# The last expert group's zeros and weights are issued by ScalarE instead of SyncE, and the steps' places are drawn anew

## The chip, the cores and the metric

The kernel runs on one core of a Trainium2 chip. The metric is the device time of one execution in microseconds (us); lower is better. The median of three runs of the kernel before is 5308.69 us (5287.12 to 5310.76).

The engines are called by their names in the profile: PE (TensorE, matmuls and transposes; PEld is its weight load), DVE (VectorE), ACT (ScalarE), POOL (GpSimd) and SP (SyncE, which only issues DMAs here). SPq and ACTq are the DMA issues of SyncE and ScalarE.

## The reference

An input x of 32 batches of 512 tokens with 256 features goes through a Mamba layer with an MLP, a layer norm, a mixture of 8 experts with the best 2 for each token and one shared expert, and a second layer norm, all in float32:

```python
def step(h, inp):                       # the scan of the Mamba layer, 16 states, 512 channels
    dt_t, B_t, C_t, x_t = inp
    dA = jnp.exp(dt_t[..., None] * A)
    h = dA * h + (dt_t * x_t)[..., None] * B_t[:, None, :]
    y = jnp.einsum('bdn,bn->bd', h, C_t)
    return (h, y)
...
h = x + _mamba(_layernorm(x, norm1_g, norm1_b), ...)
m = _layernorm(h, norm2_g, norm2_b)
attn = h + jax.nn.gelu(m @ mlp_w1.T + mlp_b1, approximate=False) @ mlp_w2.T + mlp_b2
x = _layernorm(x + attn)
...
scores = jax.nn.softmax(xf @ gate_w.T, axis=-1)
_, idx = jax.lax.top_k(scores, 2)       # each token's two experts, weighted by their scores
h = jax.nn.silu(g) * u                  # g and u: x times wg and wu of an expert
routed = ...                            # h times wd of the two experts, weighted and summed
shared = jax.nn.silu(xf @ sg.T) * (xf @ su.T) @ sd.T
x = _layernorm(x + routed + shared)
```

## The kernel before

**The order of the work.** Each engine runs one queue in program order. The work on an engine is cut into strands, generators such as `pre`, `scan`, `weigh`, `post`, `experts`, `results`, `finish` and `last`, each of which yields before each of its steps the batch to which the step belongs. `weave` (L99) merges the strands of an engine into one order by places: a step has the place 64 x batch + its entry of the table `AT` (L22), and never less than the place of the strand's step before. The tables are constants in the source. They hold for every batch, so an entry that moves does so in all 32. Places only order the steps of one engine; between the engines, semaphores decide.

**One batch** (512 tokens) goes through these steps. `pre`: sums and squares of x (ACT L698, L684), GpSimd's `normed` (L561) which gives less, ve, rs and nb of a norm, normalised tokens, their transposes, the first half of in_proj, the convolution (DVE L1218), silu, x_proj (B, C and the rank of dt), dt. B goes to DRAM (`B_rows`, L417) and comes back broadcast, one DMA for each of the 16 states (`B_spread`, L423). `scan`: for each state and each quarter of the channels, 64 times a batch, ACT computes exp(dt A) into PSUM (L755), POOL dt x B into dBx (L600, two quarters at a time), DVE runs the scan (L1229) into hs. `turn` and `weigh`: PE transposes hs into one of two PSUM banks (L974), DVE multiplies with C and adds to acc (L1245; for two of the sixteen states ACT, L768). `post`: the gate z (L991; its tanh L777, its product on DVE L1278), the sum y (L1004, L1007), w_out (L1019, L1021), mid norm, w_m1 (L1037), gelu, w_m2 (L1054), norm, the transposes of its output (L1062), the gate of the experts (L1068), the routing on DVE (L1293 to L1361), the shared expert, whose output and residual go to the DRAM buffer `shared` (ACT L825, L830), and the scatter of the tokens' rows to their experts' places in DRAM (`X_slots`, POOL L633, four indirect DMAs for the first expert and four for the second).

**The experts.** Batches form groups of 6, 6, 6, 6, 4, 2, 1 and 1 batches. When a group is scattered, `group_tiles` on DVE (L1392) writes the tiles' expert and row (`where`) and each expert's end (`ends`), 18 increments of `s_meta`. `pad` on SyncE (L434) waits for these and writes zeros behind the rows of each of the 8 experts, to an address read from `ends` into a register (L443). `all_rows` (L445) waits for the scatters and the zeros. The group's tiles of 128 rows are worked in pairs: `experts` on SyncE loads the weights (wx, L499) and the rows (xin, L505) of a pair, PE turns the rows (L1112), ACT copies them (xsT, L842), PE multiplies (L1130), ACT takes tanh (L847), DVE the products (L1373, L1376), PE the second matmul (L1145), ACT the scaled output (L858), SyncE stores it to `Y_slots` (L521). A batch has up to 12 slots for pairs (`pairs_in`); in batches 5 to 22 four or five of them are filled, with five the third slot among them.

**The finish** of a batch f needs its group's pairs done. SyncE loads `shared[f]` into the single buffer fx (L534), after waiting until batch f-1 is stored; POOL gathers the two experts' outputs into it with adding (L657, 4 and 4); ACT sums, squares and scales (L895, L684, L902) with POOL's `normed` between, and stores fx to the output (L905). The finishes of batches 27, 28 and 29 lie in the period of batch 30, those of 30 and 31 behind it.

**The last group** is batch 31 alone, with 16 tiles in 8 pairs (152 to 159, here 0 to 7). They have a buffer each (`wx_last`, `xin_last`), made of tiles that are free at the end. `last` on SyncE (L449) is one strand of 24 steps: 8 steps for the weights, the first of them with `pad` and waits for the last scans and transposes ahead; 8 for the rows, the first with `all_rows`; 8 for the outputs. `last` on PE (L1149), ACT (L861) and DVE (L1378) works the pairs staggered: the turn of a pair, the up step of the one before, the down step of the one before that. The lines of its steps are L1166, L871, L1175, L875, L1383, L1386, L1183 and L880. SyncE's loop over weights in `last` is:

```python
for q in range(NLAST):
    yield b
    if q == 0:
        pad(g)
        sp.wait_ge(s_scan, NB * STEPS)
        sp.wait_ge(s_y_turned, NB * CT)
    if q < 2:
        sp.wait_ge(s_down_e, P0 - 1 + q)
    ...
```

Of the kernel before, what the change touches and what calls it, by code (L numbers as in the profile page):

```python
# [9 lines left out]
def group_sizes(n):  # L10
# [6 lines left out]
    while n:  # L17
# [4 lines left out]
AT = {  # L22
    "ACT_experts": [124.46, 125.74, 128.8, 130.54, 134.61, 135.95, 138.86, 140.84, 142.27, 142.38, 143.71, 144.95,
        147.84, 148.99, 151.85, 153.09, 159.61, 160.41, 161.35, 163.09, 166.53, 167.41, 170.1, 171.48],
    "ACT_finish": [152.12, 152.3, 152.3, 152.68, 152.68, 152.68, 152.77, 152.92, 154.73, 155.55, 156.25, 157.25,
        167.31, 167.41, 167.41, 167.72, 167.72, 168.27, 168.27, 169.78, 170.2, 170.5, 170.5, 170.72, 197.59, 197.59,
        197.59, 197.59, 199.29, 199.63, 199.63, 199.63, 200.22, 200.22, 200.49, 200.79],
    "ACT_last": [137.32, 137.32, 137.42, 137.51, 137.53, 137.86, 139.07, 139.77, 139.77, 139.77, 139.77, 139.77,
        139.77, 140.66, 140.66, 140.66, 151.62, 151.62, 151.62, 151.86, 151.86, 151.86, 151.86, 151.86, 152.02,
        152.58, 153.06, 159.5, 162.22, 166.33, 190.88, 194.43],  # L30
    "ACT_post": [57.1, 59.75, 64.53, 68.94, 78.62, 78.62, 79.9, 80.49, 81.18, 81.28, 81.28, 81.28, 84.15, 84.15,
        84.15, 84.57, 86.17, 86.17, 87.39, 87.76, 88.72, 89.94, 97.56, 97.76, 97.76, 97.94, 99.44, 101.28, 102.72,
        103.29, 104.47, 106.02, 110.38],
    "ACT_pre": [-63.04, -63.04, -59.75, -59.75, -57.63, -54.43, -50.92, -50.92, -48.17, -32.48, -32.48, -32.48,
        -32.23, -32.01, -31.14, -25.59, -24.16, -21.01, -19.09, -15.37, -13.12, -11.61, -10.78, -8.01, -6.93, -2.89],
    "ACT_results": [126.79, 127.91, 132.04, 132.47, 136.47, 136.47, 141.6, 141.6, 142.98, 142.98, 145.52, 145.96,
        150.28, 151.15, 159.16, 159.18, 160.57, 160.89, 165.97, 165.97, 168.69, 169.98, 183.41, 185.11],
    "ACT_scan": [1.69, 3.47, 6.65, 7.28, 7.82, 7.96, 8.71, 9.61, 9.71, 10.72, 12.65, 12.65, 13.91, 14.57, 15.17,
# [4 lines left out]
    "ACT_weigh": [8.02, 10.28, 10.28, 11.04, 35.16, 36.34, 37.2, 38.03],  # L43
    "DVE_experts": [126.01, 129.67, 137.46, 140.93, 144.44, 146.06, 148.7, 153.41, 161.62, 163.32, 169.38, 174.12],
    "DVE_last": [121.51, 127.93, 156.82, 165.91, 166.45, 166.45, 183.01, 191.57],
    "DVE_meta": [106.25, 108.81, 109.84, 109.84],
    "DVE_post": [55.59, 56.79, 64.86, 67.56, 71.93, 74.38, 74.81, 75.03, 93.66, 97.97, 97.97, 97.97, 98.09, 102.46,
        103.96, 104.39, 104.39, 104.39, 104.39, 104.39, 104.39, 105.62, 105.62, 108.47],
    "DVE_pre": [-29.44, -27.59, -27.59, -25.26, -25.26, -25.26, -21.68, -21.68, -21.68, -19.08, -19.08, -18.92],
    "DVE_scan": [2.28, 3.93, 6.98, 7.82, 10.46, 10.46, 10.46, 10.46, 10.76, 11.11, 15.72, 15.72, 17.24, 17.24, 17.69,  # L50
# [4 lines left out]
    "DVE_weigh": [15.86, 16.54, 16.71, 17.85, 19.73, 19.73, 19.73, 19.73, 19.73, 19.73, 20.22, 22.1, 22.1, 25.31,  # L55
# [15 lines left out]
    "PE_turn": [8.63, 9.5, 10.6, 10.97, 11.04, 14.67, 15.36, 16.7, 19.29, 19.29, 19.87, 19.87, 20.8, 21.29, 21.32,
# [45 lines left out]
def build(nc, a, out):  # L117
# [4 lines left out]
    P = 128  # L122
# [59 lines left out]
    with ctx:  # L182
# [200 lines left out]
        def _(sp):  # L383
# [1096 lines left out]
```

## Time and profile before

| | us |
|---|---|
| median of three runs | 5308.69 |
| lowest and highest | 5287.12, 5310.76 |
| the profiled execution | 5320.7 |
| its span | 5318.9 |
| DVE busy | 4398.7 (83%) |
| PE busy | 4254.3 (80%) |
| POOL busy | 3584.5 (67%) |
| ACT busy | 3387.0 (64%) |
| DMA, mean rate | 106 GB/s |

The profile is of one execution, whose own time is 5320.7 us. A row of the timeline gives the start in us, the duration, the engine, the line, the operation, the written and the read tile, and how many instructions are merged; in brackets stands the idle time of the engine before it and what ended it. A row of the waits gives who waited for whom, the total in us, how many times, and the longest. A row of the windows gives for each engine its busy time in a stretch, the granted clock of TensorE (1 is full speed), the mean busy share of the 16 DMA engines and what they moved. Releasers are inferred from semaphores; where no one is seen, "issue" stands.

### The profile page before, as it was taken

To read this page: it belongs to the slowest core of one execution; us is meant where nothing else is said; L and a number is where in the kernel's file an instruction comes from. 1 tells how busy PE (TensorE), PEld (TensorE's weight loads), DVE (VectorE), ACT (ScalarE), POOL (GpSimd) and SP (SyncE) were. 2 spreads that over 40 slices of the span, in tenths; PEclk is the share of its full clock that TensorE was granted. 3 is DMA by queue.
4 is the path that set the end of the run, shared out by engine and by line. 5 is a ranking of instruction groups with operands and counts; after the bars stand their busy time and mean duration, and the time that the engine had idled before them with its cause. 6 is when DMAs were issued, how large, how long until landed. Compare 5 with 4: busy or idle time off the path is not lost. (4 is left out here: it accounts for less than half of the span.)

```text
span 5318.9 us, 75837 instructions
## 1 busy us (share of the span) xinstructions
PE 4254.3 (80%) x20928; PEld 2954.7 (56%) x20928; DVE 4398.7 (83%) x6313; ACT 3387.0 (64%) x6338; POOL 3584.5 (67%) x2252
## 2 busy tenths in 40 slices
PE   3777888788888888888888888888888888888872
PEld 2455555565555556555555655555555566655652
DVE  4899988988888988888888888888888888888841
ACT  4666666566666666766666766666666766766642
POOL 4666666666666667776667776667777775787743
PEclk7899998999999999989998998999998999999986
DMA  1224232233333333333233333333344442555655
GB/s 63 71 70 112 71 95 86 86 128 119 106 121 98 123 124 89 93 96 107 83 84 85 105 98 104 92 84 96 80 126 116 117 122 92 151 147 141 166 141 153
DMA packets 357156, 563.53 MB, mean 106 GB/s; under 512 B 40433, under 2 KB 203378, under 8 KB 356610
## 3 DMA queue, kind: packets, MB, share of 16 engines
q1 hardware_dynamic: 286082, 457.85, 28.2%
q0 software_dynamic: 49152, 67.27, 6.2%
q10 hardware_dynamic: 21504, 33.56, 1.7%
q8 instruction: 174, 2.85, 0.2%
q14 instruction: 244, 2.00, 0.1%
HBM read 440.66 MB, written 186.05 MB: 118 GB/s over the span
## 5 line engine op out<-in xcount | busy, mean ns | idle before, releaser
L600 POOL TENSOR_TENSOR dBx<-dtx,Bbc 128x1024 f32<-128x1024 f32 x1024 | 2431.3, 2406 | 728.6 <-DVE hs L1229 666.3
L1229 DVE TENSOR_TENSOR_SCAN hs<-ps,dBx 128x512 f32<-128x512 f32 x2048 | 2389.3, 1205 | 206.7 <-ACT ps L755 104.9
L755 ACT ACTIVATE ps<-dt,A 128x512 f32<-128x512 f32 x2048 | 1391.5, 689 | 576.6 <-DVE hs L1229 548.0
L974 PE MATMUL ps<-ident,hs 128*128 128x128 f32 x8192 | 1341.2, 304 | 507.2 <-DVE acc L1245 392.8
L974 PEld LDWEIGHTS ps<-ident,hs 128*128 128x128 f32 x8192 | 1029.3, 154 | 982.1 <-DVE acc L1245 641.1
L1245 DVE SCALAR_TENSOR_TENSOR acc<-ps,C_tok,acc 128x512 f32<-128x512 f32 x1792 | 1281.6, 738 | 284.3 <-PE ps L974 266.2
L657 POOL DMA_INDIRECT fx<-Y_slots,slots x256 | 405.0, 1582 | 126.7 <-issue 67.9
L633 POOL DMA_INDIRECT X_slots<-xs,slots x256 | 257.4, 1005 | 290.3 <-DVE slots L1361 231.9
L1130 PE MATMUL ps<-xsT,wx 128*128 128x128 f32 x2432 | 321.2, 282 | 65.0 <-ACT xsT L842 65.0
L1130 PEld LDWEIGHTS ps<-xsT,wx 128*128 128x128 f32 x2432 | 301.1, 195 | 112.7 <-issue 108.8
L1218 DVE SCALAR_TENSOR_TENSOR xc<-ps,conv_w,xc 128x511 f32<-128x511 f32 (+2 forms) x384 | 285.4, 744 | 63.5 <-ACT xc L719 50.6
L991 PE MATMUL ps<-xnT,w_in 128*128 128x512 f32 x512 | 295.7, 684 | 0.9
L939 PE MATMUL ps<-xnT,w_in 128*128 128x512 f32 x512 | 271.9, 648 | 25.9 <-DVE xc L1218 25.0
L584 POOL TENSOR_TENSOR dt<-dt,dtx 128x1024 f32<-128x1024 f32 x64 | 152.4, 2381 | 173.1 <-ACT dtx L746 173.1
L1054 PE MATMUL ps<-w_m,post_tmp 128*128 128x256 f32 x1024 | 261.8, 390 | 0.0
L1021 PE MATMUL ps<-w_out,xc 128*128 128x256 f32 x1024 | 250.4, 380 | 0.0
L1037 PE MATMUL ps<-mT,w_m 128*128 128x512 f32 x512 | 239.6, 600 | 11.1 <-ACT mT L798 10.6
L719 ACT ACTIVATE xc<-ps,conv_b,conv_w 128x512 f32<-128x512 f32 x128 | 99.0, 773 | 204.1 <-PE ps L939 201.5
L963 PE MATMUL ps<-few 16*128 16x512 f32 x256 | 181.1, 796 | 52.4 <-ACT dt L741 39.3
L1145 PE MATMUL ps<-wx,ge 128*128 128x256 f32 x608 | 171.5, 406 | 55.3 <-DVE ge L1376 53.3
L1054 PEld LDWEIGHTS ps<-w_m,post_tmp 128*128 128x128 f32 x1024 | 196.6, 197 | 27.0
L1021 PEld LDWEIGHTS ps<-w_out,xc 128*128 128x128 f32 x1024 | 192.7, 191 | 25.0
(210 smaller groups left out, 5888.2 us busy)
## 6 DMA issues: line engine op xcount, KB each, us to landing
Bbc<-B_scratch SPq DMA_DIRECT2D x512, 256.0 KB
wx<-in_experts SPq DMA_DIRECT2D x308, 384.0 KB, 5.0
Y_slots<-zeros SPq DMA_DIRECT2D x228, 256.0 KB, 4.6
xin<-X_slots SPq DMA_DIRECT2D x308, 128.5 KB, 4.1
Y_slots<-xin SPq DMA_DIRECT2D x308, 128.0 KB
xt<-in_x SPq DMA_DIRECT2D x32, 512.0 KB, 5.2
shared<-xt ACTq DMA_DIRECT2D x32, 512.0 KB
fx<-shared SPq DMA_DIRECT2D x32, 512.0 KB
```

Of the source, the lines that this page charges most:

```text
L600: pool.tensor_tensor(dBx[u % 3][:], dtx[b % 2][:, 2 * h:2 * h + 2, :], Bbc[g % NBB][:, n % CH:n % CH + 1, :].broadcast_to([P, 2, T]), ALU. ...
L657: pool.indirect_dma_start(out=fx[:, t, :], out_offset=None, in_=Y_slots[g % 2], in_offset=bass.IndirectOffsetOnAxis(ap=slots[:, f % NKEPT, ...
L755: act.activation(psA[s % 2][:], dt[b % 2][:, j, :], ACT.Exp, scale=A[:, j, n:n + 1]).then_inc(s_dA, 1)
L939: i = pe.matmul(bank(b, j)[:], w_in[:, k, j * P:(j + 1) * P], xn[:, k, :], start=(k == 0), stop=(k == KD - 1))
L974: i = pe.transpose(psH[w % 2][:, j * P:(j + 1) * P], hs[(n * CT + j) % NHB][:, t * P:(t + 1) * P], ident[:])
L991: i = pe.matmul(psG[j % 2][:], w_in[:, k, DI + j * P:DI + (j + 1) * P], xn[:, k, :], start=(k == 0), stop=(k == KD - 1))
L1021: i = pe.matmul(psG[q][:, t * D:(t + 1) * D], c[:, k, (2 * q + t) * P:(2 * q + t + 1) * P], w_out[:, k, :], start=False, stop=(k == CT - 1))
L1054: i = pe.matmul(psG[q][:, t * D:(t + 1) * D], post_tmp[:, k, (2 * q + t) * P:(2 * q + t + 1) * P], w_m2[:, k, :], start=False, stop=(k == ...
L1130: i = pe.matmul(psE[:, o * HALF + m * P:o * HALF + (m + 1) * P], w[:, m, (2 * k + o) * P:(2 * k + o + 1) * P], xsT[:, (m * KD + k) * P:(m ...
L1218: dve.scalar_tensor_tensor(out=c[:, j, s:], in0=bank(b, j)[:, 0:T - s], scalar=conv_w[:, j, NK - 1 - s:NK - s], in1=c[:, j, s:], op0=ALU.m ...
L1229: dve.tensor_tensor_scan(hs[s % NHB][:], psA[s % 2][:], dBx[s // 2 % 3][:, s % 2, :], 0.0, ALU.mult, ALU.add).then_inc(s_scan, 1)
L1245: dve.scalar_tensor_tensor(out=o, in0=psH[w % 2][:], scalar=C_tok[b % 2][:, t, n:n + 1], in1=o, op0=ALU.mult, op1=ALU.add).then_inc(s_weig ...
```

## The change

The eight weight steps of the last group leave SyncE's strand `last`, which keeps the 8 steps for the rows and the 8 for the outputs. A new strand `issue_last` on ScalarE issues the zeros and the weights of the eight pairs, with the waits that they had on SyncE (for the metadata, the last scans and transposes, and for the pairs whose buffers are taken over). The waits of `pad` for the first two groups aren't needed there. The first row step on SyncE keeps `all_rows`. DMAs, sizes and semaphores are the same.

```diff
@@ SyncE, last() @@
                 for q in range(NLAST):
                     yield b
                     if q == 0:
-                        pad(g)
-                        sp.wait_ge(s_scan, NB * STEPS)
-                        sp.wait_ge(s_y_turned, NB * CT)
-                    if q < 2:
-                        sp.wait_ge(s_down_e, P0 - 1 + q)
-                    for i in range(2):
-                        e = sp.value_load(where[g % 2][0:1, 1, 2 * q + i:2 * q + i + 1], min_val=0, max_val=NE * P)
-                        sp.dma_start(wx_last[q][:, i, :], a["experts"].rearrange("e p f -> (e p) f")[
-                            bass.ds(e, P), :]).then_inc(s_wx_last[q], 16)
-                for q in range(NLAST):
-                    yield b
-                    if q == 0:
                         all_rows(g)
@@ ScalarE @@
+            def issue_last():
+
+                g, b = NG - 1, NB - 1
+                for q in range(NLAST):
+                    yield b
+                    if q == 0:
+                        act.wait_ge(s_meta, NG * NMETA)
+                        for e in range(NE):
+                            r = act.value_load(ends[g % 2][0:1, e:e + 1], min_val=0, max_val=ROWS - P)
+                            act.dma_start(X_slots[g % 2][bass.ds(r, P), :], zeros[:, 0:ROW]).then_inc(s_padded[g % 2], 16)
+                        act.wait_ge(s_scan, NB * STEPS)
+                        act.wait_ge(s_y_turned, NB * CT)
+                    if q < 2:
+                        act.wait_ge(s_down_e, P0 - 1 + q)
+                    for i in range(2):
+                        e = act.value_load(where[g % 2][0:1, 1, 2 * q + i:2 * q + i + 1], min_val=0, max_val=NE * P)
+                        act.dma_start(wx_last[q][:, i, :], a["experts"].rearrange("e p f -> (e p) f")[
+                            bass.ds(e, P), :]).then_inc(s_wx_last[q], 16)
...
-                  (finish(), AT["ACT_finish"]), (last(), AT["ACT_last"]))
+                  (finish(), AT["ACT_finish"]), (last(), AT["ACT_last"]), (issue_last(), AT["ACT_issue_last"]))
```

All tables of `AT` have new entries. In most strands an entry moves by less than a tick or two (a batch has 64, so a tick is some 2.5 us in the loop). Those that move more: ACT_post's last entry, the shared part's last copy and its store, from 110.38 to 118.35; SP_clear's, most of which lie at 91 to 99 before and spread from -27 to 67 after; SP_B_spread's and SP_experts', by up to 14 and 10; the tables of the last group. The new table is

```python
    "ACT_issue_last": [108.86, 108.86, 113.58, 125.48, 127.66, 129.33, 129.33, 138.47],
```

From the tables the new orders follow. At the end, ScalarE has after the store of batch 28: the zeros with the weights of pairs 0, 1 and 2; the shared part's last copy and store; pair 0's copy; the weights of pairs 3 to 6; pair 0's tanh; the first pass of batch 29's finish over one tile; pair 1's copy; one output of pair 0; the rest of batch 29's finish with its store; the weights of pair 7; the other output of pair 0, and pairs 1 to 6 except for one output; batch 30's finish with that output inside; pair 7's tanh and outputs. SyncE has: fx for batch 29; the rows of pair 0; the output of pair 151; the rows of pairs 1 and 2; fx for batch 30; the rows of pairs 3 to 7; the outputs of pairs 0 to 6; fx for batch 31; the output of pair 7.

In the loop, around the steps that the prediction speaks of (places within a batch):

```
ScalarE before: scan 0, 1 | sums 2, 3 of x | tanh 3 | a square | xsT of the third slot | scan 2
ScalarE after:  scan 0, 1 | xsT of the third slot | sum 3 of x | tanh 3 | scan 2, 3 | a square
GpSimd before:  dBx 7 | rs_pre | gathers 0 to 3 | dBx 8, 9 | less_mid
GpSimd after:   dBx 7 | gathers 0, 1 | dBx 8 | rs_pre | gathers 2, 3 | dBx 9 | less_mid
TensorE before: turn 43 | turn of C, dt 0, 1 | turns 44 to 47
TensorE after:  turns 43, 44 | turn of C, dt 0, 1 | turns 45 to 47
VectorE before: weighing 35 | scans 49 to 51 | weighings 36, 37, 38
VectorE after:  weighings 35, 36 | scans 49 to 51 | weighings 37, 38
```

## Rows read from the trace of the kernel before

**Rows 1.** The page, part 1: busy us (share of the span) and instructions.
```profile
PE 4254.3 (80%) x20928; PEld 2954.7 (56%) x20928; DVE 4398.7 (83%) x6313; ACT 3387.0 (64%) x6338; POOL 3584.5 (67%) x2252
```
**Rows 2.** The windows: a batch of the loop, and 42 us near the end.
```profile
2132.80:2290.30 157.50, 129.66 (x655) 90.70 (x655) 135.76 (x191) 105.41 (x200) 111.91 (x70) 0.93 0.31 96
5193.00:5235.00 42.00, 0.00 (x0) 0.00 (x0) 2.33 (x6) 4.70 (x17) 18.09 (x18) 0.55 0.92 275
```
**Rows 3.** The waits of DVE over the whole span.
```profile
DVE acc L1245 <- PE ps L974: 266.2, 291, 4.2
...
DVE hs L1229 <- issue: 48.9, 23, 2.9
```
**Rows 4.** The timeline at the end: DVE's last metadata, then SyncE's issues.
```profile
5195.29 0.21 DVE L1434 SCALAR_TENSOR_TENSOR where<-few 1x56 int32<-1x56 f32 x1
...
5199.88 10.08 SPq L443 DMA_DIRECT2D X_slots<-zeros  x8
5210.80 4.22 SPq L462 DMA_DIRECT2D wx<-in_experts  x4
...
5229.38 3.61 SPq L473 DMA_DIRECT2D xin<-X_slots  x4
...
5241.56 0.33 SPq L534 DMA_DIRECT2D fx<-shared  x1
...
5282.98 0.37 SPq L534 DMA_DIRECT2D fx<-shared  x1
```
**Rows 5.** The timeline at the end, GpSimd: the gathers of batches 29, 30, 31.
```profile
5204.27 1.65 POOL L657 DMA_INDIRECT fx<-Y_slots,slots  x1 [0.30 <-issue]
...
5245.10 1.65 POOL L657 DMA_INDIRECT fx<-Y_slots,slots  x1 [8.80 <-DMA fx<-shared]
...
5288.11 1.65 POOL L657 DMA_INDIRECT fx<-Y_slots,slots  x1 [11.72 <-DMA Y_slots<-xt]
```
**Rows 6.** The timeline at the end, ScalarE.
```profile
5230.05 0.42 ACT L895 ACTIVATE fx<-fx 128x256 f32<-128x256 f32 x1 [36.39 <-DMA fx<-Y_slots,slots]
...
5238.43 0.38 ACTq L905 DMA_DIRECT2D out<-fx  x1
...
5278.53 0.38 ACTq L905 DMA_DIRECT2D out<-fx  x1
...
5279.68 0.38 ACT L875 ACTIVATE Bbc<-ps 128x256 f32<-128x256 f32 x1
```
**Rows 7.** The timeline of batch 31's last stage, ScalarE and TensorE.
```profile
5169.67 1.93 ACT L810 ACTIVATE xs<-ps,nb_post,rs_post 128x256 f32<-128x256 f32 x4
5173.58 0.38 ACT L847 ACTIVATE ge<-ps 128x256 f32<-128x256 f32 x1 [1.99 <-PE ps L1130]
...
5175.89 1.85 PE L1068 MATMUL ps<-w_gate,mT 128*128 128x8 f32 x16
```
**Rows 8.** The timeline of a batch in the loop, DVE.
```profile
2296.67 1.60 DVE L1245 SCALAR_TENSOR_TENSOR acc<-ps,C_tok,acc 128x512 f32<-128x512 f32 x2 [1.37 <-PE ps L974]
...
2330.53 0.69 DVE L1278 SCALAR_TENSOR_TENSOR post_tmp<-post_tmp,ps 128x512 f32<-128x512 f32 x1 [0.46 <-ACT post_tmp L777]
...
2359.02 1.22 DVE L1229 TENSOR_TENSOR_SCAN hs<-ps,dBx 128x512 f32<-128x512 f32 x1 [2.46 <-issue]
...
2381.15 1.41 DVE L1245 SCALAR_TENSOR_TENSOR acc<-ps,C_tok,acc 128x512 f32<-128x512 f32 x2 [4.01 <-PE ps L974]
```
**Rows 9.** The same batch, TensorE and ScalarE.
```profile
2329.65 0.76 PE L1112 MATMUL ps<-ident,xin 128*128 128x128 f32 x4
2329.90 0.60 ACT L777 ACTIVATE post_tmp<-ps 128x512 f32<-128x512 f32 x1 [4.82 <-PE ps L991]
```
**Rows 10.** The same batch, GpSimd.
```profile
2328.59 0.23 POOL L564 TENSOR_SCALAR less_pre<-total_pre 128x4 f32<-128x4 f32 x1
...
2355.00 1.54 POOL L657 DMA_INDIRECT fx<-Y_slots,slots  x1 [0.30 <-issue]
...
2360.60 0.84 POOL L564 TENSOR_SCALAR less_mid<-total_mid 128x4 f32<-128x4 f32 x1
```

More of the change, by code:

```diff
@@ new lines @@
+    "ACT_issue_last": [108.86, 108.86, 113.58, 125.48, 127.66, 129.33, 129.33, 138.47],
+    "ACT_last": [120.8, 129.48, 132.8, 132.8, 140.06, 140.06, 140.06, 140.06, 140.06, 140.06, 144.33, 144.33, 145.09,
+        145.09, 145.09, 145.09, 146.05, 146.05, 146.05, 147.5, 147.5, 147.5, 147.5, 152.04, 152.04, 152.04, 152.04,
+        152.84, 154.53, 177.03, 185.79, 216.32],
+    "ACT_post": [57.35, 60.94, 66.45, 69.45, 79.46, 80.48, 80.85, 80.85, 81.54, 81.54, 81.63, 81.63, 85.73, 85.76,
+        85.76, 85.86, 86.13, 86.17, 87.26, 87.37, 90.05, 90.28, 98.27, 98.28, 98.28, 98.79, 100.24, 101.17, 102.43,
+        103.34, 104.52, 105.28, 118.35],
@@ new lines @@
+    "ACT_pre": [-61.74, -60.71, -60.71, -59.06, -57.03, -52.13, -49.49, -49.49, -48.63, -33.35, -33.35, -32.88,
+        -32.09, -31.87, -30.81, -25.82, -24.3, -21.33, -18.98, -16.07, -12.99, -11.91, -10.59, -7.87, -4.8, -2.4],
+    "ACT_results": [127.3, 127.3, 132.11, 132.76, 136.44, 137.11, 140.7, 141.55, 143.03, 143.03, 145.69, 145.99,
+        150.81, 151.11, 156.67, 157.61, 160.99, 161.07, 166.64, 166.64, 168.94, 169.13, 183.53, 186.53],
+    "ACT_scan": [3.35, 3.35, 6.67, 6.67, 7.8, 8.3, 9.45, 10.02, 10.17, 10.39, 11.25, 11.68, 14.09, 14.55, 15.02,
[4 rows of a table added]
@@ new lines @@
+    "ACT_weigh": [9.62, 10.14, 10.98, 12.16, 34.9, 35.32, 36.68, 39.27],
+    "DVE_experts": [124.98, 128.25, 135.67, 140.22, 144.28, 145.73, 148.72, 152.81, 160.53, 164.54, 168.59, 178.42],
+    "DVE_last": [183.29, 201.28, 215.47, 220.99, 278.92, 290.11, 324.13, 400.13],
+    "DVE_meta": [107.83, 109.9, 110.62, 110.71],
+    "DVE_post": [56.67, 56.67, 66.11, 68.98, 72.58, 72.79, 74.19, 74.26, 94.15, 98.28, 98.28, 98.36, 98.66, 102.41,
+        104.19, 104.19, 104.35, 104.55, 104.55, 104.55, 104.55, 104.8, 105.34, 107.97],
@@ new lines @@
+    "PE_inputs": [120.96, 124.78, 133.68, 138.5, 140.02, 145.42, 148.2, 150.87, 158.74, 163.96, 167.6, 173.15],
+    "PE_last": [196.77, 215.96, 235.49, 241.39, 241.39, 241.39, 241.39, 241.39, 241.39, 250.71, 250.71, 251.91,
+        251.91, 251.91, 255.3, 255.3, 264.79, 399.1, 403.58, 404.4, 404.4, 404.4, 405.8, 405.8],
+    "PE_post": [53.17, 53.2, 54.7, 56.71, 60.13, 60.13, 60.55, 69.16, 71.25, 71.64, 73.22, 74.64, 75.58, 76, 76.54,
+        79.17, 80.58, 80.58, 80.99, 81.58, 86.02, 86.13, 86.35, 86.35, 86.35, 87.3, 87.3, 87.3, 87.82, 87.82, 90.91,
+        90.91, 91.07, 92.55, 92.55, 97.96, 99.02, 99.24, 100.49, 100.84, 102.99, 103.26, 103.26, 105.95, 106.08,
+        106.34, 106.34, 109.11],
@@ new lines @@
+    "PE_pre": [-32.68, -30.39, -29.4, -28.51, -24.84, -24.84, -23.37, -23.37, -20.65, -19.2, -18.08, -15.28, -15.09,
+        -12.86, -11.58, -11.58, -11.54, -11.14, -8.25],
+    "PE_results": [124.4, 130.09, 135.79, 139.63, 144.19, 147.99, 150.26, 155.29, 163.38, 166.14, 170.12, 181.83],
+    "PE_turn": [8.98, 10.08, 10.57, 10.76, 10.76, 13.08, 13.31, 16.17, 19.53, 19.61, 19.99, 20.13, 20.18, 21.24,
[4 rows of a table added]
+    "POOL_finish": [141.99, 142.37, 143.47, 143.47, 144.65, 148.59, 149.05, 149.05, 152.46, 155.37, 156.96, 157.05,
+        158.6, 158.6, 163.17, 163.17, 164.71, 164.71, 166.68, 167.3, 177.48, 177.73, 186.61, 186.61, 189.03, 189.4,
+        189.85, 189.86, 197.6, 198.69],
@@ new lines @@
+    "POOL_post": [79.9, 80.78, 99.06, 103.1, 103.49, 103.49, 103.57, 106.03, 106.03, 106.14, 106.81, 106.81],
+    "POOL_pre": [-69.93, -48.91, -0.18, 3.17],
+    "POOL_scan": [3.05, 6.11, 12.86, 13.4, 13.4, 13.87, 13.87, 13.87, 14.47, 15.49, 19.69, 22.43, 26.99, 27.7, 28.01,
+        28.01, 28.68, 28.93, 32.33, 32.53, 35.09, 35.13, 35.42, 39.04, 41.28, 42.96, 46.94, 51.63, 57.03, 59.01,
+        59.01, 59.66],
+    "SP_B_rows": [-7.47],
+    "SP_B_spread": [-7.3, -5.69, 7.16, 9.7, 12.47, 18.83, 18.83, 24.66, 30.53, 37.79, 39.2, 47.59, 47.59, 47.59,
+        50.96, 51.13],
@@ new lines @@
+    "SP_behind": [-33.08, 228.6, 399.93],
+    "SP_clear": [-26.84, -0.12, 24.86, 25.02, 25.24, 25.24, 35.7, 35.7, 36.37, 38.92, 38.92, 38.92, 38.92, 38.92,
+        48.86, 55.84, 65.77, 65.77, 67.1],
+    "SP_experts": [117.42, 125.4, 133.26, 137.66, 139.93, 151.58, 152.75, 163.22, 164.94, 170.55, 170.55, 178.43],
+    "SP_finish": [142.46, 165.42, 180.14],
+    "SP_inputs": [-65.67],
+    "SP_last": [123.7, 125.48, 135.29, 142.89, 184.53, 193.78, 195.56, 195.56, 195.56, 195.56, 196.79, 197.96,
+        197.96, 197.96, 197.96, 228.99],
@@ L96 @@
+    "SP_results": [136.68, 139.23, 142.7, 152.4, 158.17, 162.99, 164.98, 169.45, 172.94, 178.32, 187.99, 188.85],
 }
```

68 lines of the change are left out of this document (10 added, 58 removed), and 30 rows, old and new, of the table AT.

## The prediction

> **What bounds the kernel now.** I read the page's busy line first [rows 1]: VectorE (DVE) is busy 4398.7 us of 5318.9, TensorE 80% of the span, ScalarE 64%, GpSimd 67%. Then the stretches [rows 2]. In the loop VectorE is busy 135.76 of 157.5 us, so in a batch about 22 us are lost to waits and nothing but these can be won. In 5193 to 5235 us VectorE and TensorE do nothing, and the DMA engines are 92% busy at 275 GB/s: this is the stretch from which the change takes issues. The waits of VectorE say what the lost time in the loop is: mostly the wait of a weighing (L1245) for its transpose in PSUM (L974), 266.2 us in 291 waits [rows 3].
>
> Then the end. SyncE issues the eight zeros from 5199.88, the sixteen weights from 5210.80, and the first rows at 5229.38 [rows 4]; this looks like 30 us in front of the last group. But it isn't what ends last. The chain of waits at the end is a chain over one buffer, fx: gathers of batch 29 from 5204.27 on GpSimd, behind the scatters of batch 31, the last of which is issued by 5203.97 [rows 5]; ScalarE starts on it at 5230.05 and stores it at 5238.43; only then SyncE loads fx for batch 30 (5241.56), which ScalarE stores at 5278.53; only then fx for batch 31 (5282.98), whose gathers start at 5288.11 [rows 4 to 6]. About 40 us a batch, one after the other, whatever the expert pairs do. The last eight pairs run beside it.
>
> **Part 1, the issues.** Eight zeros cost SyncE 10.08 us, 1.26 each; four weights 4.22, so 1.06 each, and with the waits and registers between them sixteen take 5229.38 - 5210.80 = 18.6 us, 1.16 each [rows 4]. I find no dynamic-address issue on ScalarE in the trace, so I take SyncE's price, with one and a half times it as the upper bound and no lower price. In the new order ScalarE meets the zeros after the store of batch 28, and can start when VectorE has written the last group's metadata, 5195.5 [rows 4]; in the profile it waits 36.39 us until 5230.05, from 5193.7 on [rows 6]. Ahead of batch 29's first pass it has eight zeros and the weights of seven pairs: 10.1 + 14 x 1.16 = 26.3 us, plus the shared store, a copy and a tanh, some 2.3 us: from 5195.5 to about 5224. That is hidden, with 6 us to spare. At one and a half times the price it isn't: +7 us. Queued behind these issues on ScalarE: the last copy of batch 31's shared part with its store (read only at 5282.98), pair 0's copies, batch 29's finish.
>
> SyncE, freed of it, can issue the first rows when zeros and scatters have landed, which I put 5 us after 5203.97, near 5209, instead of 5229.38. But the new places let only three pairs' rows go ahead of fx for batch 30; the other five stay behind it, where they were. And ScalarE's new order has nearly all of batch 29's finish ahead of pairs 1 to 7. The pairs then go on at about 5242 in either kernel, and the last pair's tanh stands behind the store of batch 30 in both (5278.53 and 5279.68 in the trace [rows 6]). What the pairs can give is at most the gap between the earliest that fx for batch 31 can be there and 5288.11. From a store to the next load are 5241.56 - 5238.43 = 3.1 us and from the load to the first gather 5245.10 - 5241.56 = 3.5, so 5278.53 + 6.6 = 5285.2 [rows 4 to 6]: 2.9 us.
>
> Against it: one copy (0.6) and one output (0.4) of the last pairs come to lie inside batch 29's finish, +1.0. In batch 31's last stage the new order has pair 150's tanh (5173.58) ahead of the four normalised outputs that start at 5169.67 and take 1.93 us; the gate's matmuls at 5175.89 need them [rows 7]. The tanh ends at 5173.96, the outputs then at 5175.9, and with some 1.3 us for the transposes and copies between, which partly overlap, the gate comes near 5177.2: +1.3 us, and scatter, gathers and all behind follow. More DMA in the full stretch, at 92% [rows 2], may make batch 29's gathers land later: three pairs' rows are six issues of 128 KB, 0.8 MB, at 275 GB/s 2.9 us; I take 0.7. Part 1: +3 us, between -2.9 and +10.
>
> The Trainium skill ("DMA: Bandwidth & Descriptors", Issuing engines are not separate DMA queues) says that SyncE's, ScalarE's and GpSimd's DMAs run on the same 16 engines and interleave, and that issuing from several saves only issue time. It speaks against the change where the transfers bound the stretch; by it the rows couldn't land 20 us sooner as a whole, since the share is 0.92 already. The sum doesn't hang on it.
>
> **Part 2, the new places.** They move the steps of all 32 batches, and 1% there outweighs the end. Most pairs of neighbours keep their order; where they swap I looked at whether VectorE waits there in the trace.
> (a) At 2296.67 VectorE waits 1.37 us for a transpose [rows 8] that TensorE does behind the small transposes and matmuls of the next batch's dt. The new order has one transpose ahead of these and one weighing ahead of three scans: about -0.7 us a batch. Three weighings that come to stand together before the third tanh product take off about 0.5 (waits of 0.5 us at that place). With 31 batches, -37 us; the other bound is 0, if the time is waited for elsewhere.
> (b) In batches that have a pair in the third slot, the new order of ScalarE copies that pair's turned rows (xsT) before the fourth sum of x and the fourth tanh; the old one does these first. TensorE turns the rows at 2329.65, just behind the matmul for which the tanh waits 4.82 us [rows 9]. So tanh and sum come after 0.6 + 0.6 us of other work and after the turn; VectorE's product at 2330.53 waits 1 us or more, and GpSimd's less_pre (2328.59) [rows 10], which stands before the second dBx, 2 us. By hand, step by step with the durations of the trace, the gated products come 1.9 us later. It is passed on: through w_out, the mid norm and w_m1 to the weighing that waits 4.01 us at 2381.15 [rows 8] for TensorE. There are 15 batches with such a wait of 4.0 us (first at 1140, last at 4988): +28.5 us; bounds 0 and 2.9 each.
> (c) GpSimd issues four gathers before the ninth dBx (the last at 2355.00, [rows 10]); a scan at 2359.02 waits 2.46 us for it [rows 8]. In the new order two of the four come after it. There are 15 such waits (2.4 to 2.9 us, together 40; the waits put down to no releaser are 48.9 in all [rows 3]). But the mid norm's less_mid (2360.60) still has all four gathers and both dBx ahead of it, and VectorE waits for what comes out of that at 2381.15. I take 0: saved at 2359, waited for at 2381.
> (d) SyncE's clears of the first twelve batches are spread; VectorE shows no wait for them: 0. Pair loads stand behind more broadcasts of B; by the trace the load of 2358 would go at 2364 and is needed at 2374: 0.
>
> **The sum.** -37 + 28.5 + 3 = -5.7 us on the profiled execution (5320.7, of which the span is 5318.9): 5315.0. That execution is 12.0 above the median of the three runs, 5308.69, so 5303.
>
> **Rivals.** (R1) Slower: the copy ahead of the tanh costs its full price and (a) gives nothing. 15 x 2.9 + 8 = +51, 5360. It decides as soon as ScalarE reaches that copy before TensorE's turn of the pair has ended (2330.4 in the trace); for it: ScalarE idles 4.82 us just there [rows 9], so it is early. Against: a third of it at least is absorbed by waits that exist already. (R2) Faster: the 40 us of (c) aren't given back, as the mid norm's chain has slack that I don't see: 5303 - 40 = 5263. Against: 4.01 us at 2381.15. (R3) The end works as the text of the change suggests: first rows 20 us sooner, and the span with them, 5303 - 3 - 20.7 = 5279. Against it the fx chain, in which no pair stands until 5288. (R4) ScalarE issues at the same moments as SyncE did, because the metadata it waits for is late: no change in the end at all, 5300.
>
> **How the numbers follow.** My forecast has 0.42, R1 0.28, R2 0.20, R3 0.05, R4 0.05. About half a per cent, 26.5 us, is what a measurement of this kernel can tell from no change. Faster: R2 and R3, 0.25. Same: forecast and R4, 0.47. Slower: R1, 0.28. The forecast's own range is 5266 to 5335 ((a) and (b) at their bounds partly against each other); that of 8 in 10 goes most of the way to R1 and R2: 5252 to 5358.
>
> **What would show it.** Right: zeros on ScalarE from about 5195 and no later start of batch 29's first pass than 5233; first rows on SyncE near 5209; 35 to 42 us between the stores of batches 29, 30 and 31; the wait of 2.4 us before the scan gone and that of 4 us longer; the fourth tanh behind xsT. Wrong: a period of steady batches off 157.4 us by more than 1 us; ScalarE still issuing when batch 29's gathers have landed; a wait of VectorE over 2 us at a place where none is now.

## The result, and the profile after

The changed kernel takes 5337.85 us (median of 9 runs, 5333.27 to 5345.98) against 5316.53 of before (9 runs, 5287.12 to 5319.05): ratio 1.0051, 95% interval 1.0037 to 1.0065. The medians differ by 21 us; a ratio of 1.0051 is 27. That is small, but clear of the spread of the runs. I had put the median at 5303 and the likeliest sign at "no change"; 5337.85 lies above the forecast's own range (5266 to 5335) and inside the wide one (to 5358). Its profiled execution took 5340.87 us with a span of 5339.0.

The page of the changed kernel, part 1, and its waits of DVE (columns as in [rows 3]: total us, times, longest). Lines of the old file from L462 on stand 8 to 11 lines elsewhere: the scan is L1237, the weighing L1253, the turn L982.
```profile
PE 4290.3 (80%) x20928; PEld 2931.6 (55%) x20928; DVE 4394.3 (82%) x6313; ACT 3394.1 (64%) x6338; POOL 3588.8 (67%) x2252
```
```profile
DVE acc L1253 <- PE ps L982: 402.4, 265, 5.0
DVE ge L1381 <- ACT ge L836: 113.2, 72, 13.7
...
DVE hs L1237 <- ACT ps L744: 53.3, 68, 2.8
```
VectorE does the same work, 4394.3 us against 4398.7 [rows 1]. What grew is its waits for TensorE's turns: 402.4 us against 266.2 [rows 3]. Part of it replaces other waits of VectorE: the 48.9 us of scans released by nothing that the profile shows [rows 3] have nearly gone, and those for ScalarE's exp in PSUM (L755, now L744) have halved, from 104.9 to 53.3 us.

Where in the batch? VectorE's 2048 scans are a ruler: scan k of batch b is the same work in both kernels. Adding VectorE's idle times between the same scans gives, per batch (before, after): batches 1 to 6, 12.1 and 15.0; 7 to 12, 15.1 and 16.7; 13 to 24, 20.4 and 21.2; 25 to 30, 25.0 and 21.6. So the changed kernel loses in the first 24 batches and wins 3.4 us a batch in six of the last: its loss of 21 us is what remains of a larger one. Two stretches lose over most of the batches: scans 20 to 23 (5.6 and 6.6 us in batches 13 to 24) and scans 52 to 55 (1.7 and 3.7 us in batches 1 to 6, 0.8 and 2.9 in batches 13 to 24). In batches 13 to 24 scans 12 to 15 win 2.6 us and scans 16 to 19 lose 1.9; this is step (c), given back behind the scan as in e6 below. The first is the stage of w_m1, here in batch 3; first before, then after.
```profile
395.03 1.04 PE L974 MATMUL ps<-ident,hs 128*128 128x128 f32 x8
396.15 3.67 PE L1037 MATMUL ps<-mT,w_m 128*128 128x512 f32 x8
...
400.29 1.41 DVE L1245 SCALAR_TENSOR_TENSOR acc<-ps,C_tok,acc 128x512 f32<-128x512 f32 x2 [2.10 <-PE ps L974]
```
```profile
400.25 1.02 PE L1045 MATMUL ps<-mT,w_m 128*128 128x512 f32 x2
401.79 3.67 PE L1045 MATMUL ps<-mT,w_m 128*128 128x512 f32 x8 [0.52 <-ACT post_tmp L792]
405.30 1.04 PE L982 MATMUL ps<-ident,hs 128*128 128x128 f32 x8
...
405.94 2.25 DVE L1253 SCALAR_TENSOR_TENSOR acc<-ps,C_tok,acc 128x512 f32<-128x512 f32 x3 [4.15 <-PE ps L982]
```
Before, two turns (x8) stand ahead of the last eight matmuls of w_m1 and VectorE has two weighings to do meanwhile; after, only one does, turn 17 stands behind all of them, and VectorE waits 4.15 us instead of 2.10. After, the wait is 4.1 to 4.4 us in every batch from 1 to 30. Before, it is 2.10 or 1.93 us in 16 of them and 4.01 us, nearly as long, in the other 14.

The second, behind scan 54 of batch 4 in the changed kernel: TensorE, then VectorE.
```profile
779.44 2.07 PE L971 MATMUL ps<-few 16*128 16x512 f32 x2
781.44 4.33 PE L999 MATMUL ps<-xnT,w_in 128*128 128x512 f32 x6
785.61 1.04 PE L982 MATMUL ps<-ident,hs 128*128 128x128 f32 x8
```
```profile
786.25 1.41 DVE L1253 SCALAR_TENSOR_TENSOR acc<-ps,C_tok,acc 128x512 f32<-128x512 f32 x2 [3.05 <-PE ps L982]
```
Three half steps of z (L999, x6) stand ahead of turn 48; the old order has one ahead of it and two behind. They take 4.33 us here, where TensorE is at its lower clock for most of them. In batch 10 of the same kernel, at full clock, six such matmuls take less, and VectorE's wait is 0.61 us:
```profile
1710.60 2.84 PE L999 MATMUL ps<-xnT,w_in 128*128 128x512 f32 x6
```
The windows (columns: us, busy and count of PE, PEld, DVE, ACT, POOL, granted clock, DMA share, GB/s), first three of before, batches 3 and 4, then one of after, batch 4:
```profile
613.00:619.40 6.40, 5.24 (x16) 3.21 (x17) 4.58 (x6) 4.24 (x7) 6.38 (x4) 0.51 0.22 75
752.00:756.60 4.60, 2.00 (x10) 0.84 (x9) 4.52 (x6) 3.81 (x8) 4.10 (x4) 0.98 0.53 194
757.00:770.00 13.00, 13.00 (x30) 6.44 (x31) 8.68 (x10) 6.05 (x10) 9.74 (x5) 0.50 0.31 111
```
```profile
775.00:785.70 10.70, 10.70 (x23) 4.71 (x22) 6.80 (x8) 6.43 (x11) 6.27 (x3) 0.56 0.52 167
```
In each batch of both traces the clock falls to half (0.5, 1.2 of 2.4 GHz) behind dt's chain, in which TensorE idles two or three times for 0.3 to 1.4 us. It comes back after 3 to 7 us in some batches and after 10 to 14 in others. VectorE's waits from scan 48 to 55 follow it: up to 3 us in the first case, 4 to 6 in the second. I call a batch slow when VectorE waits over 3 us between scans 51 and 56. Of batches 1 to 31, 11 are slow in the profiled execution of before and 22 in that of the changed kernel. A slow batch of before has such waits too, 0.95 and 2.73 us in batch 4.

The end. Stores of batches 28, 29 and 31 on ScalarE, before (those of 29 and 30 are in [rows 6]) and then after, with the zeros and the first weights:
```profile
5192.64 0.38 ACTq L905 DMA_DIRECT2D out<-fx  x1
...
5315.56 0.38 ACTq L905 DMA_DIRECT2D out<-fx  x1
```
```profile
5212.67 0.38 ACTq L913 DMA_DIRECT2D out<-fx  x1
5216.55 10.00 ACTq L859 DMA_DIRECT2D X_slots<-zeros  x8
5227.43 3.56 ACTq L866 DMA_DIRECT2D wx<-in_experts  x4
...
5260.21 0.41 ACTq L913 DMA_DIRECT2D out<-fx  x1
...
5298.61 0.41 ACTq L913 DMA_DIRECT2D out<-fx  x1
...
5335.59 0.41 ACTq L913 DMA_DIRECT2D out<-fx  x1
```
From the store of batch 28 to the last one are 122.92 us in both. The last scan starts at 5093.0 before and 5109.5 after: 16.5 us are lost by there, 3.5 between it and the store of batch 28, none behind.

### The profile page after: what moved, and what is told of

Its sections match the earlier page's. It is cut to its first block and busy times, and to the rows that moved or that the text cites. A ratio compares the mean times of both kernels' runs of the same rounds, so it can differ in the third digit from the quotient of the medians.

```text
span 5339.0 us, 75835 instructions
## 1 busy us (share of the span) xinstructions
PE 4290.3 (80%) x20928; PEld 2931.6 (55%) x20928; DVE 4394.3 (82%) x6313; ACT 3394.1 (64%) x6338; POOL 3588.8 (67%) x2252
## 5 line engine op out<-in xcount | busy, mean ns | idle before, releaser
L1237 DVE TENSOR_TENSOR_SCAN hs<-ps,dBx 128x512 f32<-128x512 f32 x2048 | 2394.1, 1207 | 112.1 <-ACT ps L744 53.3
L744 ACT ACTIVATE ps<-dt,A 128x512 f32<-128x512 f32 x2048 | 1402.2, 690 | 791.4 <-DVE hs L1237 758.5
L982 PE MATMUL ps<-ident,hs 128*128 128x128 f32 x8192 | 1325.8, 296 | 556.5 <-DVE acc L1253 379.5
L1253 DVE SCALAR_TENSOR_TENSOR acc<-ps,C_tok,acc 128x512 f32<-128x512 f32 x1792 | 1283.5, 739 | 425.6 <-PE ps L982 402.4
L982 PEld LDWEIGHTS ps<-ident,hs 128*128 128x128 f32 x8192 | 997.3, 150 | 1016.2 <-DVE acc L1253 592.2
L947 PE MATMUL ps<-xnT,w_in 128*128 128x512 f32 x512 | 290.0, 686 | 51.5 <-DVE xc L1226 50.6
L999 PE MATMUL ps<-xnT,w_in 128*128 128x512 f32 x512 | 313.8, 735 | 0.1
```

Source lines behind the costliest of these rows:

```text
L744: act.activation(psA[s % 2][:], dt[b % 2][:, j, :], ACT.Exp, scale=A[:, j, n:n + 1]).then_inc(s_dA, 1)
L947: i = pe.matmul(bank(b, j)[:], w_in[:, k, j * P:(j + 1) * P], xn[:, k, :], start=(k == 0), stop=(k == KD - 1))
L982: i = pe.transpose(psH[w % 2][:, j * P:(j + 1) * P], hs[(n * CT + j) % NHB][:, t * P:(t + 1) * P], ident[:])
L999: i = pe.matmul(psG[j % 2][:], w_in[:, k, DI + j * P:DI + (j + 1) * P], xn[:, k, :], start=(k == 0), stop=(k == KD - 1))
L1237: dve.tensor_tensor_scan(hs[s % NHB][:], psA[s % 2][:], dBx[s // 2 % 3][:, s % 2, :], 0.0, ALU.mult, ALU.add).then_inc(s_scan, 1)
L1253: dve.scalar_tensor_tensor(out=o, in0=psH[w % 2][:], scalar=C_tok[b % 2][:, t, n:n + 1], in1=o, op0=ALU.mult, op1=ALU.add).then_inc(s_weig ...
```

## The experiments

A single profiled execution can't price half a per cent: the kernel before alone ran between 5283.22 and 5332.81 us over the series. Ratios are those of the timed runs, traces serve to find places. Every edit is in the tables of places (indices from 0), unless said.

**e1, the issues alone.** New issue code, all places of before:
```diff
-    "SP_last": [114.9, 115.98, 115.98, 117.93, 117.93, 119.24, 123.52, 133.25, 133.25, ...
+    "SP_last": [133.25, ...
+    "ACT_issue_last": [111, 111, 111, 111, 111, 111, 111, 111],
```


> The change's issue code (eight zeros and sixteen weight issues on ScalarE, right behind the last copy of batch 31's shared part) with all places of before. Theory 1 (the end is the chain over fx, and the issues are worth nothing there): ratio to before 1.000 (0.999 to 1.001), first rows on SyncE near 5209 to 5213 instead of 5229.38, stores of batches 29 and 30 within 3 us of 5238.4 and 5278.5. Theory 2 (the issues themselves lengthen the end; the changed kernel lost 7.8 us behind its last broadcast of B): ratio 1.0015, store of batch 29 five or more us later. Rival R3 of the prediction (the issues shorten the end): ratio 0.996.

Measured 1.0013 (0.9994 to 1.0031). This rules out R3 but can't tell theory 1 from theory 2; the trace can. ScalarE and SyncE of this run:
```profile
5169.31 0.38 ACTq L914 DMA_DIRECT2D out<-fx  x1
...
5173.97 10.01 ACTq L860 DMA_DIRECT2D X_slots<-zeros  x8
5184.77 3.60 ACTq L867 DMA_DIRECT2D wx<-in_experts  x4
...
5200.28 1.39 ACTq L867 DMA_DIRECT2D acc<-in_experts  x2
...
5215.80 0.41 ACTq L914 DMA_DIRECT2D out<-fx  x1
...
5291.87 0.38 ACTq L914 DMA_DIRECT2D out<-fx  x1
```
```profile
5190.28 3.68 SPq L463 DMA_DIRECT2D xin<-X_slots  x4
```
The first rows go 21.0 us behind the store of batch 28, where before had 36.7 ([rows 4] and 5192.64): 15.8 us sooner. The last store is 122.56 us behind it, before 122.92. Sixteen microseconds of earlier rows buy 0.4, as theory 1 says: the chain over fx sets the end. In the changed kernel the first rows go 17.8 us behind that store (5230.50), and the last store still 122.92.

**e2, the places alone.** The code of before, the new places, the eight weight issues on SyncE where before has them.

> The new places with zeros and weights still issued by SyncE, ahead of the last rows. Theory 1 (all of the loss is in the places: 12 us in the loop and 4 to 8 us in batch 31's last stage, where a tanh of pair 150 stands ahead of the normalised outputs): ratio to before 1.004 to 1.005, like the changed kernel. Theory 2 (the end's 7.8 us come from the issues): ratio 1.0023.

Measured 1.0084 (1.0056 to 1.0111): the whole loss and rather more. Its interval meets those of the changed kernel, so I don't read a gain of the issues out of the difference.

**e3 and e4, one number each in the changed kernel.**
```diff
-    PE_turn[17] = 24.2
+    PE_turn[17] = 22.67
```


> The changed kernel with one number changed: TensorE's turn 17 of each batch goes right behind turn 16, as in before, ahead of the five half steps of w_m1 that stand between them now. Theory 1 (VectorE's wait of 4.15 us for this turn in every batch is the price of that order; it was 2.10 us): the wait falls to about 2.1 and the kernel is 31 x 0.5 to 31 x 1.0 us faster than the changed one, as the mean loss around this place is 0.4 to 1.0 us a batch: ratio to before 0.999 to 1.002. Rival (the time is waited for again a few steps on, at the scans behind the mid norm): ratio unchanged at 1.005, with the wait moved.

```diff
-    PE_turn[48] = 55.04
+    PE_turn[48] = 53.18
```


> The changed kernel with one number changed: TensorE's turn 48 of each batch goes ahead of the second and third half of the post norm's product z (as in before) instead of behind all three. Theory 1 (VectorE waits 3.0 to 4.5 us for it in every batch behind scan 54, where before had 0.95 and in some batches 2.7 more; mean loss there 1.9 us a batch): about 30 to 45 us faster than the changed kernel, ratio to before 0.997 to 0.999. Rival (the halves of z that are done later are waited for by the second last scans of the batch and nothing is won): ratio 1.004 to 1.006.

Measured 1.0031 (1.0015 to 1.0046) and 1.0025 (1.0009 to 1.0041). Both are below the changed kernel's 1.0051 by some 10 to 15 us, less than expected: e4 was to bring 30 to 45, and e3's ratio lies above the forecast 0.999 to 1.002. In e3 the wait fell from 4.15 to 3.49 only, since VectorE's order around it is still the new one, and the idle between scans 20 and 23 stayed (4.4 us against 4.2 in batches 1 to 6). e4's waits between scans 51 and 56 fell by 15 us in the trace with 21 batches still at over 3 us.

**e5, both.** 

> The changed kernel with both numbers of TensorE's places changed (turn 17 right behind turn 16, turn 48 ahead of two halves of z). Alone they brought 12 and 17 us. Theory 1 (two separate causes, and together they hold most of the loss of the changed kernel): ratio to before 0.999 to 1.001. Theory 2 (both act through one thing, the clock that TensorE is granted while it turns the states of scans 46 to 56; whatever shifts the batch may bring it back): no better than the better of the two, ratio 1.002 to 1.003, and the number of batches with more than 3 us of VectorE waits between scans 51 and 56 stays near 20 of 31 (11 in before, 22 in the changed kernel).

Measured 1.0013 (1.0001 to 1.0025), which is nearest to theory 1 (up to 1.001), while 23 batches were slow. So the two numbers bring back most of the loss, and not through that count.

**e14, e15, e16, the converse: the same two orders put into the kernel before.**
```diff
-    PE_turn[17] = 23.22
+    PE_turn[17] = 24.8
```


> The kernel before with one number changed: TensorE's turn 17 goes behind the half steps of w_m1 that in the changed kernel stand ahead of it. Theory 1 (this order is a cause): VectorE's wait behind scan 21 is longer by 2 us or more in every batch, ratio 1.002 to 1.005 if half of it is given back. Theory 2 (any shift of the loop moves it as much; the orders are no causes): ratio 0.999 to 1.001.

```diff
-    PE_turn[48] = 54.49
+    PE_turn[48] = 54.9
```


> The kernel before with one number changed: TensorE's turn 48 goes behind the third half of z, as in the changed kernel, where undoing it brought 17 us. Theory 1 (this order is a cause, dear where TensorE is at half clock): waits between scans 51 and 56 longer by 0.5 us at full clock and by 1 to 2 us in batches at half clock, ratio 1.002 to 1.004. Theory 2: ratio 0.999 to 1.001.

> Both numbers of the last two runs together. Theory 1: their sum, ratio 1.004 to 1.008, which would be the whole loss of the changed kernel or more. Theory 2: 0.999 to 1.001.

**e17, the changed kernel again, on the same chip.**

> The changed kernel itself, for a ratio from the same chip and hour as the three others. Expected 1.0051, as before; if it is below 1.003, then part of the loss that the other runs were measured against was of that chip or hour.

| | ratio to before | 95% interval |
|---|---|---|
| e14, turn 17 late | 1.0030 | 1.0004 to 1.0056 |
| e15, turn 48 late | 1.0019 | 1.0001 to 1.0038 |
| e16, both late | 1.0059 | 1.0038 to 1.0080 |
| e17, the changed kernel | 1.0068 | 1.0046 to 1.0091 |

Two numbers out of several hundred make the kernel before nearly as slow as the changed one. In e14 the wait of batch 3 is
```profile
409.08 2.25 DVE L1246 SCALAR_TENSOR_TENSOR acc<-ps,C_tok,acc 128x512 f32<-128x512 f32 x3 [2.75 <-PE ps L975]
```
0.65 us longer than before, less than the 2 us that I expected, and 0.9 us a batch come up anew between scans 28 and 31 in batches 1 to 6. The profiled executions of e14 and e16 have only 5 and 7 slow batches although both kernels are slower, so these two orders don't act through that count. The count does go with the table: 4 to 14 slow batches in the nine traces with the old places, up to single moves, and 20 to 28 in the seven with the new ones (e9, e2 to e5 and the changed kernel twice). What it costs net isn't shown, since e5 has 23 and a ratio of 1.0013. Nor does a trace show where e16's 31 us arise: its profiled execution was the fastest of its seven, 5324.36 us against a median of 5338.95.

**e6, step (c) alone in the kernel before.**
```diff
-    POOL_scan[8] = 12.02
+    POOL_scan[8] = 11.31
```


> The kernel before with one number changed: on GpSimd the ninth dBx goes ahead of the third and fourth gather (step (c) of the prediction alone). Prediction: the 15 waits of 2.4 us before the scan vanish and the time is waited for at the 4.0 us wait behind it: ratio 1.000 (within 0.001). Rival R2: 40 us are won, ratio 0.9925.

Measured 1.0003 (0.9990 to 1.0015). VectorE in batch 15:
```profile
2360.14 0.42 DVE L1374 SCALAR_TENSOR_TENSOR ge<-ge,ps 128x256 f32<-128x256 f32 x1 [2.59 <-ACT ge L848]
...
2381.64 2.34 DVE L1230 TENSOR_TENSOR_SCAN hs<-ps,dBx 128x512 f32<-128x512 f32 x2 [4.85 <-ACT ps L756]
...
2392.51 1.41 DVE L1246 SCALAR_TENSOR_TENSOR acc<-ps,C_tok,acc 128x512 f32<-128x512 f32 x2 [4.01 <-PE ps L975]
```
The wait of 2.46 us [rows 8] is gone. The same pair of scans that waited 1.35 us for ScalarE in before, three scans on, now waits 4.85 us; ScalarE is in the mid norm there. Given back, though at another instruction than the one I named: the 4.01 stays as it is.

**e7, part of step (b) in the kernel before.**
```diff
-    ACT_experts[4:6] = 134.61, 135.95
+    ACT_experts[4:6] = 132.89, 135.31
```


> The kernel before with two numbers changed: on ScalarE the copy of the turned rows of a pair in the third slot goes ahead of the fourth tanh and the fourth sum of x (step (b) of the prediction alone). Prediction: 1.9 us in each of 15 batches, +28.5 us, ratio 1.0054, the wait of 4.0 us at weighings behind scan 21 longer by 1.9. Rival 1: the full price, 1.008. Rival 2, from the changed kernel, where that wait is 4.4 with this order: nearly nothing, ratio 1.000 to 1.001.

Measured 1.0010 (0.9992 to 1.0029). ScalarE and VectorE, batch 15:
```profile
2333.64 0.60 ACT L843 ACTIVATE xsT<-ps 128x512 f32<-128x512 f32 x1 [3.95 <-PE ps L1113]
2334.14 0.59 ACT L778 ACTIVATE post_tmp<-ps 128x512 f32<-128x512 f32 x1
```
```profile
2334.76 0.69 DVE L1279 SCALAR_TENSOR_TENSOR post_tmp<-post_tmp,ps 128x512 f32<-128x512 f32 x1 [0.54 <-ACT post_tmp L778]
```
The copy does come first, and VectorE's product waits 0.54 us where it waited 0.46 [rows 8]. It stands 5.17 us behind the weighing ahead of it (at 2329.59 here), against 5.55 before. But the edit did less than the expectation says: all four sums of x still stand ahead of the copy, while in the changed kernel one of them stands between the copy and the tanh. Batch 15 isn't the whole either. VectorE's waits for this tanh, over the whole trace, before, e7 and changed kernel:
```profile
DVE post_tmp L1278 <- ACT post_tmp L777: 4.7, 10, 0.7
DVE post_tmp L1279 <- ACT post_tmp L778: 15.9, 20, 1.6
DVE post_tmp L1286 <- ACT post_tmp L766: 13.9, 21, 1.4
```
They grow by 9 to 11 us in all, not by 28.5, and the 4.01 us at the weighing stay (2384.46). The price of (b) isn't 1.9 us a batch.

**e8, turn 49 of before earlier** (PE_turn[48] and [49] = 54.69). With 54.69 turn 48 stands where it stood, between the first and second half step of z (53.8 and 54.7); only turn 49 moves, ahead of two of them.

> The kernel before with two numbers changed: TensorE's turns 48 and 49 go ahead of the second half of the post norm's z; before has turn 48 between the first and second half and turn 49 behind the third. Theory 1 (each half of z ahead of a turn is waited for by VectorE behind scan 54, 0.95 us at full clock and 2.7 more where the clock is half): the waits there fall by 1 us in all batches and by 2 to 3 in the slow ones, ratio 0.991 to 0.995. Rival (turns that are early only change which matmul waits; z is needed by the product that ends the batch's weighings, and the time is waited for there): ratio 0.998 to 1.001.

Measured 1.0003 (0.9989 to 1.0018): the rival. A turn later cost time in e15, the next turn earlier wins none here.

**e9, the tanh of pair 150 behind the outputs again in the changed kernel** (ACT_experts[19] = 163.09 for 161.6).

> The changed kernel with one number changed: the tanh of pair 150 (batch 31's last stage) goes behind the four normalised outputs on ScalarE again. From the last broadcast of B to the first scatter of the last group the changed kernel takes 6.7 us longer than before. Theory 1: this tanh, which there waits 3.8 us for TensorE, is 4 us of them; scatters, gathers and the stores of batches 29, 30 and 31 then come 4 us sooner after the last broadcast. Rival (TensorE's and VectorE's orders of the stage set it): under 1 us.

One execution, 5378.67 us, span 5376.8. ScalarE in batch 31's last stage:
```profile
5228.21 1.93 ACT L799 ACTIVATE xs<-ps,nb_post,rs_post 128x256 f32<-128x256 f32 x4
5232.14 0.38 ACT L836 ACTIVATE ge<-ps 128x256 f32<-128x256 f32 x1 [2.00 <-PE ps L1138]
```
The outputs now start 5.19 us behind the last statistics (5223.02), in the changed kernel 8.45 (5188.25 behind 5179.80): the tanh cost the end 3 to 4 us, as theory 1 says. But this number holds for that slot in all batches, and in those with pairs VectorE's idle between scans 36 and 39 grew from 0.0 to 1.0 us. So the new place of this tanh seems to be a gain in the loop that I had not counted; a single time can't say how large.

**e10 and e12, whole regions put back.** All engines' places between 20.5 and 31 as in before, and in e12 TensorE's and VectorE's between 51 and 63 too.

> The changed kernel with the places of all engines that lie between 20.5 and 31 of a batch as in before (the stage of w_m1 and w_m2). Turn 17 alone brought 10 us but left the waits between scans 20 and 24 as they were (4.2 to 6.6 us a batch against 3.6 to 5.6 in before), as VectorE's order there stayed the new one. Theory 1: with VectorE's order undone too, these waits are those of before and the kernel is 20 to 25 us faster than the changed one, ratio to before 1.001. Rival (the difference is a matter of later stages and of the clock): ratio 1.003, as with turn 17 alone.

> As the one before, and TensorE's and VectorE's places between 51 and 63 as in before as well. Theory 1 (the order of the three halves of z against the turns decides in how many batches TensorE is at half clock behind scan 52): the batches with over 3 us of waits between scans 51 and 56 fall from 20 or more to about 11 of 31, and with what the change gains elsewhere (GpSimd and the batches from 25 on) the kernel beats before: ratio 0.995 to 0.998. Rival (which batches are slow comes from farther ahead, where these places stay new): 20 slow batches, ratio 1.000 to 1.001.

Measured 1.0208 (1.0189 to 1.0227) and 1.0653 (1.0632 to 1.0675). In batches 1 to 6, without pairs, e10's waits between scans 16 and 31 are those of before (4.5 us, changed kernel 5.0). In batches with pairs the mixture makes new ones: 8.3 us between scans 20 and 23, where the changed kernel has 6.6. In e12 VectorE waits 9 us a batch behind scan 48. Both are far above all that was expected (at most 1.003), so neither theory is tested; the edits were too coarse.

**e13, TensorE kept busy.** Into before's code, ahead of its waits for dt's small copy and for the first relu, one matmul each (the first with a wait of its own for its PSUM bank):
```diff
+                        pe.matmul(psG[0][:], w_in[:, 0, 0:P], xn[:, 0, :], start=True, stop=True)
```


> The kernel before with two matmuls of 512 columns more in each batch, whose results nobody reads: one ahead of TensorE's wait for dt's small copy, one ahead of its wait for the first relu of dt, where it idles 1.06 and 1.36 us. In before its clock falls to half right behind these idles and stays there 6 us in 20 batches and 13 us in 11. Theory 1 (the fall comes of these idles, and the slow batches' 3.3 us of waits come of the fall): no fall there, no wait over 3 us between scans 51 and 56, 36 us won from the 11 slow batches and up to 1 us in each of the others: ratio 0.987 to 0.993. Rival 1 (the clock falls anyway, as it is not these two idles): waits as in before, ratio 1.000 to 1.003. Rival 2 (the fall moves to another place of the batch and costs there): ratio 0.998 to 1.002 with fewer slow batches.

Measured 0.9998 (0.9979 to 1.0017). In its trace the lower clock behind dt's chain remains in most batches (0.80 between scans 48 and 55, as before), 4 batches are slow instead of 11, and five show 1.00 there. In batch 4 the idles are down to 0.20, 0.33 and 0.30 us, and the clock falls all the same:
```profile
761.00:774.00 13.00, 13.00 (x30) 6.38 (x30) 8.46 (x10) 5.87 (x10) 9.52 (x5) 0.50 0.40 111
```
Rival 1 or 2. So these idles aren't shown to be what brings the clock down, and what the clock costs in all stays open.

## Why the prediction was wrong, point by point

- **What bounds the kernel** held: VectorE and its waits in the loop, the chain over fx at the end.
- **Part 1, the issues.** +3 us, between -2.9 and +10: e1 gives +7, between -3 and +16, and its trace -0.4 behind the store of batch 28. ScalarE's price is SyncE's: 1.25 us a zero against 1.26; weights 0.89 to 0.95 each within a group of four against 0.90 to 1.06. Zeros began 4.7 us behind the store of batch 28 (e1), first rows 21.0 behind it, where I had 16 (5209 less 5192.64). The tanh ahead of the outputs was right in kind and mis-sized: 1.3 predicted, 4.0 measured (8.45 us from statistics to outputs against 4.43 before, 5169.67 less 5165.24), since the tanh itself waited 3.80 us for TensorE.
- **The rule on shared DMA engines.** In e1 the stretch of 42 us that starts 0.36 us behind the store of batch 28, as that of [rows 2] does, has zeros and weights from one queue and rows from another. It shows a DMA share of 0.91 at 282 GB/s, before 0.92 at 275:
```profile
5169.67:5211.67 42.00, 1.08 (x4) 0.71 (x4) 2.33 (x6) 4.40 (x16) 17.87 (x16) 0.55 0.91 282
```
  A second queue moved hardly more. By the Trainium skill ("DMA: Bandwidth & Descriptors", Issuing engines are not separate DMA queues) the DMAs of all issuing engines interleave on the same 16 engines; the trace agrees.
- **(a), -37 us: the step that failed.** The gain between scans 48 and 51 exists in part: there the changed kernel idles 0.3 to 0.5 us less a batch. But I weighed only the swaps at places where before already waited and took the others at nothing. Two of these, turn 17 behind w_m1 and turn 48 behind three half steps of z, cost 31 us together (e16, 0.59% of 5311; 20 to 42). That these two orders cost it is shown in both directions, by e16 and e5; through which waits is argued from the two places above.
- **(b), +28.5 us: the second failure.** For the part that it moved e7 allows -4 to +15 us, and VectorE's waits for the tanh grew by 9 us in the changed kernel. I added up durations behind one another; in the trace most of the 1.9 us aren't there, as the product stands 5.17 us behind its weighing and not later than before (5.55). Its error, by luck, hid part of that of (a): the sum, 5315.0 for the profiled execution, is 26 us short of 5340.9.
- **(c), 0** held (e6, and scans 12 to 19 of the changed kernel: 2.6 us won and 1.9 lost), though the time was waited for at a scan in the mid norm and not at 2381. **(d), 0** wasn't tried alone; nothing in the traces speaks against it.
- **Rivals.** R1 had the right side, with 51 us for 21, for the wrong reason; R2 falls with e6, R3 with e1. R4 isn't what happened (the issues did move), though the end behind batch 28 is as long as it says; its 5300 is missed. The case that came true, a loss by TensorE's order in the stages of w_m1 and z, wasn't among them.
- **What would show it wrong** did: "a wait of VectorE over 2 us at a place where none is now" is the 3.05 us for turn 48 at 786.25. Two thirds of the batches have one of this kind; before waited at most 0.95 us for this turn, and in its 11 slow batches once more, for the next one.

Left open: e16 is below e17 by 0.0009, less than either interval, so the rest of the change may cost -10 to +20 us; what the changed kernel's slow batches cost and its batches 25 to 30 win, which no run takes apart; and how much of the two orders' price is TensorE's lower clock.

## What to carry to other kernels

In a static order of steps, price each swap by what now stands ahead of whom, above all transposes that the bounding engine waits for behind matmuls that nobody waits for; a place without a wait today can still get one. Test such an order by single moves, undone in the new kernel and made in the old: both directions together show a cause, while whole regions put back break more than they tell. Ask of an issue that is freed early whether its transfer is on the last chain; here 16 us sooner bought nothing.

## What the hardware showed

TensorE's clock fell to half behind idles of at most 1.4 us in dt's chain, in e13 behind idles of at most 0.33 us there. In one batch it stayed there with TensorE busy throughout (13.00 of 13.00 us), in others for half as long or less, with the same program. The same kernel's time spread over 0.9% (5283 to 5333 us). ScalarE issued DMAs with an address from a register as fast as SyncE (1.25 and 1.26 us a zero).
